# Selection and first token group of a Mamba block with routed experts: constants shared, score halves made by ScalarE, tie mask added inside the scan, second group's statistics and normalisation placed later

## The reference, cut to what matters

```
scores = softmax(xf @ gate_w.T)                 # 16384 x 8
vals, idx = top_k(scores.T, k)                  # k = 2048 tokens for each expert
y = layernorm(xf[idx]) * ln_w + ln_b
h = gelu(y @ fc1[e].T + b1[e])                  # 256 -> 1024
out = (h @ fc2[e].T + b2[e]) * vals             # 1024 -> 256
xf = xf.at[idx].add(out)                        # then residual and layer norm
```

## Time and profile before

| | us |
|---|---|
| median of 3 runs | 4371.68 (4365.58 to 4371.81) |
| the profiled execution, its own time | 4374.49 |
| its span, first to last instruction | 4372.8 |

### The profile page before, as it was taken

The page is one execution under the profiler, slowest core; times in us unless marked ns, Lnnn a source line. Parts: engine busy times, 40 slices in busy tenths (PEclk is TensorE's granted clock), DMA queues, the critical chain, the costliest instruction groups (busy, mean ns, idle before and its releaser), DMA issues. The chain is left out here.

```text
span 4372.8 us, 58015 instructions
## 1 busy us (share of the span) xinstructions
PE 3537.1 (81%) x19574; PEld 2473.3 (57%) x19574; DVE 3740.1 (86%) x4783; ACT 3508.6 (80%) x5979; POOL 3496.0 (80%) x1785
## 2 busy tenths in 40 slices
PE   7778888888888878888888887878865499999990
PEld 3455555555555555555555555555554488888870
DVE  5899999999999999999999999999996666666535
ACT  5889989899999999999999999999871355656646
POOL 3899999999899999999999999999892355555543
PEclk9999999999999999999999999999975699999995
DMA  2667766777666777777766666777662233333328
GB/s 86 152 161 172 170 165 165 174 163 166 162 161 158 172 174 170 172 168 163 178 165 164 164 161 160 171 177 167 158 155 44 72 64 61 63 64 63 61 33 309
DMA packets 184229, 626.30 MB, mean 143 GB/s; under 512 B 33904, under 2 KB 99568, under 8 KB 128640
## 3 DMA queue, kind: packets, MB, share of 16 engines
q0 software_dynamic: 74688, 366.52, 42.7%
q1 hardware_dynamic: 104640, 239.32, 16.5%
q10 hardware_dynamic: 4608, 16.78, 1.0%
HBM read 221.47 MB, written 68.68 MB: 66 GB/s over the span
## 5 line engine op out<-in xcount | busy, mean ns | idle before, releaser
L464 POOL TENSOR_TENSOR dbu<-du,bb 128x2048 f32<-128x2048 f32 x511 | 2432.7, 4813 | 103.1 <-DVE h L940 78.1
L940 DVE TENSOR_TENSOR_SCAN h<-da,hlast,dbu 128x512 f32<-128x512 f32 x1536 | 1869.0, 1266 | 84.0 <-POOL dbu L464 59.3
L792 PE MATMUL ht<-ident,h 128*128 128x128 f32 x8192 | 1178.9, 289 | 461.1 <-DVE h L940 175.9
L525 ACT ACTIVATE da<-dl,negA 128x512 f32<-128x512 f32 x2048 | 1414.0, 702 | 122.7 <-DVE h L940 116.8
L792 PEld LDWEIGHTS ht<-ident,h 128*128 128x128 f32 x8192 | 966.8, 148 | 876.2 <-DVE h L940 320.9
L544 ACT ACTIVATE pair<-ht,ct 128x512 f32<-128x512 f32 x896 | 592.0, 688 | 128.4 <-DMA acc<-pair 70.7
L940 DVE TENSOR_TENSOR_SCAN h<-da,dbu 128x512 f32<-128x512 f32 x512 | 593.1, 1208 | 43.7 <-POOL dbu L464 23.1
L716 PE MATMUL spare<-xin,win 128*128 128x512 f32 x1024 | 495.4, 614 | 11.4 <-DMA xin<-in_xt 7.3
L725 PE MATMUL spare<-xh,conv 128*128 128x512 f32 x1024 | 463.8, 595 | 0.8 <-ACT xh L556 0.8
L1559 ACT ACTIVATE hraw<-f,b 128x512 f32<-128x512 f32 x256 | 176.3, 688 | 261.0 <-PE f L1617 245.2
L1488 POOL DMA_INDIRECT sums<-ot,idx x128 | 205.2, 1603 | 212.7 <-DVE ot L1789 180.3
(11 more groups left out here) (219 smaller groups left out, 5611.5 us busy)
## 6 DMA issues: line engine op xcount, KB each, us to landing
acc<-pair POOLq DMA_DIRECT2D x222, 1024.0 KB, 7.4
bb<-b_rows SPq DMA_DIRECT2D x128, 1024.0 KB, 6.6
acc<-acc POOLq DMA_DIRECT2D x64, 1024.0 KB, 8.0
dl<-du POOLq DMA_DIRECT2D x62, 512.0 KB, 5.8
xin<-in_xt SPq DMA_DIRECT2D x32, 512.0 KB, 4.9
x_scores<-xres SPq DMA_DIRECT2D x32, 512.0 KB, 4.6
sums<-xres SPq DMA_DIRECT2D x32, 512.0 KB, 6.4
rows<-sums SPq DMA_DIRECT2D x32, 512.0 KB, 6.2
```

The source lines that it names most:

```text
L464: pool.tensor_tensor(dbu[n % 2][:], du[q][:], bb[part % 2][:, m:m + 1, :].to_broadcast([P, DT, CH]), ALU.mult).then_inc(dbu_done, 1)
L525: act.activation(da[DA_SLOT[m]][:], dl[q][:, dt, :], ACT.Exp, scale=negA[:, dt, n:n + 1]).then_inc(exp_done, 1)
L792: last = te.transpose(ht[HT_SLOT[m]][:, dt * P:(dt + 1) * P], h[n % 2][:, dt, b * P:(b + 1) * P], ident[:])
L940: dve.tensor_tensor_scan(h[n % 2][:, dt, :], da[DA_SLOT[n * DT + dt]][:], dbu[n % 2][:, dt, :], start, ALU.mult, ALU.add).then_inc(scan_do ...
```

## The change

1. **Shared constants.** The identity of `stage1` is allocated in `program` and used by all stages. The index patterns are made by GpSimd in `stage2`, behind `ones`, and cast by GpSimd. To make room in SBUF the tiles of the first stage's end (`lg_end` and its partners) lie on `hlast` and `lg`. `count_hi` is a copy of 16 columns of `count`.
2. **Score halves by ScalarE.** `stage2` gets a ScalarE stream that copies the upper halves in two pieces of 512, each as soon as its half of `sc` is there. VectorE waits for both.
3. **Tie mask in the scan.** VectorE's `gt + eq` goes. The scan adds `eq` and `gt` itself; GpSimd computes `chosen = gt + eq`, which the place computation (`run`) now waits for.
4. **Sums apart, slots by halves.** The product for `tot[:, 1:2]` runs during the first scan, and the first half of the slots is taken when four of the eight transposes are back.
5. **First group.** `first_issued` is raised by a memset on GpSimd's engine. VectorE splits only `w1` before the statistics, `w2` after. For group 0 VectorE adds the epsilon and computes `shift`, GpSimd only the power; ScalarE normalises tiles 0 and 1, VectorE 2 and 3; ScalarE writes `yt_upper` and VectorE `yt`.
6. **Second group.** `row_stats(1)`, `variance(1)` and `list_rhs(1)` come behind `rest_of_input(0)` on VectorE. ScalarE normalises group 1 after the second gelu part of step 0 instead of before the first.

```
--- before.py
+++ after.py
         a = Alloc(nc, ctx)
-        ident = a.sb("ident", [P, P])
+        ident = d["ident"]
...
-        lg_end = a.sb("lg_end", [P, 2 * NB, 8])
-        mx_end = a.sb("mx_end", [P, 2 * NB])
-        ssum_end = a.sb("ssum_end", [P, 2 * NB])
+        lg_end = hlast[:].rearrange("p n k -> p (n k)").rearrange("p (b e) -> p b e", b=2 * NB)
+        mx_end, ssum_end = lg[:, 0, :], lg[:, 1, :]
...
             @block.gpsimd
             def _(pool):
-                pool.memset(ident[:], 0.0).then_inc(made, 1)
                 pool.memset(same[:], 1.0).then_inc(made, 1)
                 pool.wait_ge(made, 1)
-                pool.sem_inc(passed, 1)
-                pool.affine_select(out=ident[:], in_=ident[:], compare_op=ALU.not_equal, fill=1.0, base=0,
-                                   pattern=[[-1, P]], channel_multiplier=1).then_inc(ident_ok, 1)
...
                 pool.memset(ones[:], 1.0).then_inc(const_ok, 1)
+                pool.iota(counti[:], [[1, P]], base=0, channel_multiplier=0).then_inc(iotas, 1)
+                pool.iota(blki[:], [[1, SL], [SL, G]], base=0, channel_multiplier=0).then_inc(iotas, 1)
+                pool.iota(pidi[:], [[0, 1]], base=0, channel_multiplier=1).then_inc(iotas, 1)
+                pool.wait_ge(iotas, 3)
+                pool.tensor_copy(d["count"], counti[:].unsqueeze(2).to_broadcast([P, P, 2]))
+                pool.tensor_copy(d["blk"], blki[:])
+                pool.tensor_copy(d["pid"], pidi[:])
+                pool.tensor_scalar(d["count_hi"], counti[:, 0:16].unsqueeze(2).to_broadcast([P, 16, 2]), float(HI), None,
+                                   ALU.mult)
+                pool.wait_ge(chain, 6)
+                pool.tensor_tensor(chosen[:], gt[:], eq[:], ALU.add).then_inc(chosen_ok, 1)
+
+            @block.scalar
+            def _(act):
+                halves = sc[:].bitcast(BF16).rearrange("p (j two) -> p j two", two=2)
+                for h in range(2):
+                    act.wait_ge(sc_ok, h + 1)
+                    act.copy(sc_upper[:, h * 512:(h + 1) * 512], halves[:, h * 512:(h + 1) * 512, 1]).then_inc(upper_ok, 1)
...
+                te.wait_ge(chain, 1)
+                te.wait_ge(mats, 2)
+                te.matmul(tot[:, 1:2], same[:], cnt[:], start=True, stop=True).then_inc(sums, 1)
                 te.wait_ge(chain, 3)
-                te.wait_ge(mats, 2)
-                te.matmul(tot[:, 1:2], same[:], cnt[:], start=True, stop=True)
                 te.matmul(tot[:, 2:3], before[:], run[:, J - 1:J], start=True, stop=True).then_inc(sums, 1)
...
                 dve.wait_ge(sc_ok, 2)
-                halves = sc[:].bitcast(BF16).rearrange("p (j two) -> p j two", two=2)
-                dve.tensor_copy(sc_upper[:], halves[:, :, 1]).then_inc(sc_ok, 1)
-                dve.wait_ge(sc_ok, 3)
+                dve.sem_inc(passed, 1)
+                dve.wait_ge(upper_ok, 2)
...
                 dve.wait_ge(chain, 6)
-                dve.tensor_tensor(gt[:], gt[:], eq[:], ALU.add).then_inc(chain, 1)
-                dve.wait_ge(chain, 7)
-                dve.tensor_tensor_scan(pos[:], ones[:], gt[:], 0.0, ALU.mult, ALU.add).then_inc(chain, 1)
-                dve.wait_ge(sums, 2)
+                dve.tensor_tensor_scan(pos[:], eq[:], gt[:], 0.0, ALU.add, ALU.add).then_inc(chain, 1)
+                dve.wait_ge(sums, 3)
                 dve.tensor_copy(off[:], tot[:, 3:4]).then_inc(chain, 1)
-                dve.wait_ge(chain, 9)
-                dve.scalar_tensor_tensor(run[:], pos[:], off[:], gt[:], ALU.add, ALU.mult).then_inc(chain, 1)
-                dve.wait_ge(back, SL)
+                dve.wait_ge(chain, 8)
+                dve.sem_inc(passed, 1)
+                dve.wait_ge(chosen_ok, 1)
+                dve.scalar_tensor_tensor(run[:], pos[:], off[:], chosen[:], ALU.add, ALU.mult).then_inc(chain, 1)
                 for s in range(0, SL, 4):
+                    dve.wait_ge(back, s + 4)
                     last = dve.tensor_scalar(slot[:, s * P:(s + 4) * P], big[s // 4][:], -1.0, None, ALU.add)
...
                 def prologue():
                     gather(0, 0, 0)
-                    pool.sem_inc(first_issued, 1)
+                    pool.memset(nmean[:], 0.0).then_inc(first_issued, 1)
                     gather(0, 1, 0)
-                    rstd_and_shift(0)
+                    pool.wait_ge(first_var, 1)
+                    pool.sem_inc(pool_passed, 1)
+                    pool.tensor_tensor(rstd[:], ve[:], half[:], ALU.pow).then_inc(rstd_ok, 1)
                     gather(0, 2, 0)
                     rstd_and_shift(1)
...
                         last.then_inc(gelu_ok, 1)
+                        if m == 1 and grp == 0:
+                            normalise(1, 1)
...
                     dve.wait_ge(first_issued, 1)
                     split_weights(0, 0, 0)
-                    split_weights(0, 0, 1)
                     row_stats(0, 0, 0)
                     variance(0)
+                    dve.wait_ge(st, 2)
+                    dve.tensor_scalar(ve[:], mv[:, :, 1], LN_EPS, None, ALU.add).then_inc(first_var, 1)
+                    dve.wait_ge(rstd_ok, 1)
+                    dve.scalar_tensor_tensor(shift[:], mv[:, :, 0], -1.0, rstd[:], ALU.mult, ALU.mult
+                                             ).then_inc(shift_ok, 1)
                     dve.wait_ge(shift_ok, 1)
...
+                    last.then_inc(xn_dve, 1)
+                    split_weights(0, 0, 1)
+                    dve.wait_ge(small_in, 32)
...
+                    dve.wait_ge(yt_dve, 2)
+                    rest_of_input(0)
                     row_stats(1, 0, 1)
                     variance(1)
-                    rest_of_input(0)
+                    list_rhs(1)
                     list_onehot(1, 0)
```

114 lines of the change are left out of this document (65 added, 49 removed).

## The result

| | before | changed |
|---|---|---|
| median (lowest to highest), 7 runs each | 4371.21 us (4363.17 to 4373.31) | 4355.73 us (4349.33 to 4360.57) |
| ratio, 95% interval | | 0.9973 (0.9964 to 0.9982) |
| profiled execution: own time, span | 4374.49, 4372.8 | 4351.39, 4349.7 |

The account below looks back on a forecast made before the run. Selection and prologue were taken as bound by one dependent chain, the rest by TensorE from the first products; 2.7 us in the selection plus 4.3 in the prologue gave 7.0, so 4367.5 profiled, 4364.7 median, range 4360 to 4370.

Parts of the forecast that it names:

- stages without an edit: First stage: tiles move in SBUF, same instructions, costed at nothing; the last stage got no term.
- 2 us of spread: Whole time: runs of before spread over 6 us, so a median can be 2 us off; this entered the range.
- First compares: Start of selection: collision with GpSimd keeps 0.7 us lost and adds 0.3; bounds 0.7 better, 1.0 worse; place gains 2.2.
- Sums apart: Selection after the search: VectorE waits for one product instead of two; gain 0.4 us.
- tie mask: Selection's scan: addition goes, but the scan holds up GpSimd's `chosen`; cost 0.5 us, bounds +1.2 and -0.7.
- Slots: End of selection: the first half of the slots runs during the last four transposes; gain 0.6 us.
- patterns: Third stage's prologue: VectorE's first table no longer waits for index patterns; gain 1.7 us.
- Issues and norm: Prologue, group 0: first four issues gain 2.9 us, second four cost 2.3, norm gains 1.5, shared normalisation 1.0.
- that rival: Prologue: weight splits do not stretch the gather issues; sum 5.7 us, time 4366.0; chance 0.05.
- Second group: Third stage's first products: normalisation moved behind the second gelu part loses 0.5 us, between 0 and 2.1; `shift` after 5.
- the slower rival: First products: TensorE's standstill keeps the clock at 1.2 GHz; a whole first stretch would give 4406 us; chance 0.03.
- A chance: Whole time: chance 0.3 of faster by over 0.2%, from half the no-hold-up case and a fifth to a quarter of the main.

Follow-up runs that it names:

- e3_norm_first: The changed kernel with ScalarE's normalisation of the second group's slot put back ahead of the first gelu part; one execution took 4363.43 us.
- same_again: The changed kernel sent once more without any edit; median 4356.26 us, ratio 0.9967 to the kernel before.

## Why the prediction was wrong

- **The step that failed: stages without an edit were costed at nothing, and the base was given 2 us of spread.** The prediction says of the first stage that its instructions are the same, "and I cost that at nothing", and has no term for the last stage. The medians lie 15.5 us apart, not 7.0. Of this the last stage gave 2.1 to 2.5 us by the place of ScalarE's code. The row was in the trace of before: a first transfer of 2.85 us beside others of 0.34. The edits that I costed gave 6.2 to 6.8 us up to `ot` against 7.0, so they were over-, not underrated. The remaining 7 us by the medians (3 to 6 by the ratios) lie in no stretch behind `packed`, and their cause is open. The traces show only that the first stage moves by 18 us from execution to execution, so that a range with 2 us of spread was too narrow; as far as this surplus is scatter of the base, the miss is bad luck and not a mechanism.
- **First compares: the size of a term failed too.** I kept the 0.7 us that were lost before and added 0.3 for the collision. It is 2.05 us (3.33 against 1.28), twice that: 1.4 us worse than before, where 1.0 was the bound. The 42 memsets of `digits`, not priced at all, now fall there and hold the first compare for 1.27 us. The place gives 2.6 - 1.4 = 1.2 us, not 2.2.
- **Sums apart and tie mask: right in mechanism.** `chosen` ended 2.14 us after the scan's end where 2.5 was written, VectorE stood before the places, and undoing the two SBUF operands freed it. From `eq`'s end to the second `run` it is 4.49 us, 4.46 before: the loss of 0.5 came out at nothing, by 2.14 for 2.5 and shorter hand-overs. With the sums' 0.4, `gt` to `run` gained 0.4 where -0.1 was the sum.
- **Slots, patterns: right.** 0.6 and 1.7, each shown alone, against 0.6 and 1.7.
- **Issues and norm: right in sum.** First product 3.2 us nearer to the first gather, against 2.9 - 2.3 + 1.5 + 1.0 = 3.1. The splits do stretch the issues (2.97 and 2.89 us), so that rival falls. Undoing that part alone costs 1.6 us.
- **Second group: 0.3 to 1.0 lost against 0.5.** TensorE stood still 1.40 us before 3445.06, waiting for `hidden_upper`; the granted clock was 1.00 on both sides of it, so the slower rival falls for this change, while e3_norm_first shows it at work behind 4.86 us. The spread of 0.6 goes with the moment at which the clock rises: in the changed kernel twelve products of 0.63 us come before it, in same_again six. `shift` came 6.0 us after the first product, not 5, since GpSimd's two short steps took 1.00 and 1.17 us beside VectorE's tables. I had not seen that the move avoids 4 us.
- **The base.** The forecast was taken off the median 4371.68. By the marks the kernel before should stand at 4366.6, and where its 3 to 5.5 us above that come from is open.
- **A chance.** Half of 0.2 and a fifth to a quarter of 0.6 make 0.22 to 0.25 for a gain of over 0.2%, not 0.3.

With the 8.4 us that repeat, the time from the same base would have been 4363.3, within the range; the rest of the miss is not explained by any step.

## What to carry to other kernels

Cut each execution at marks and compare stretch by stretch: executions of one kernel agreed within 0.3 to 0.8 us behind the first stage and differed by 8 us in it, so a 2 us edit is read from one profile, stretch by stretch, and a whole time can't show it. Give a term, or at least a spread, to stages that the diff leaves alone. When a step moves forward in time, list what else stands at its new place: small memsets and a row of ones on GpSimd cost 2.05 us where 2.6 were gained, and waits put them into gaps for nothing. Before adding helper work that reads SBUF on GpSimd beside a VectorE instruction with two SBUF operands, see whether an idle engine can put one of them into PSUM.
